# A graph network's first layer on one core: VectorE's mask, hits, small numbers and edge sources in a PSUM bank, and one bank for all sums by edge

## The reference, cut to what matters

```python
def _L0_gnn_ref(inp, edge_row, edge_col, edge_val, kernel, bias):
    support = jnp.matmul(inp, kernel)
    messages = edge_val[:, None] * support[edge_col]
    output = jax.ops.segment_sum(messages, edge_row, num_segments=N_NODES)
    return output + bias
...
x = _layernorm(x + _L0_gnn_ref(x, src, dst, edge_weight, L0_gnn_kernel, L0_gnn_bias), axis=-1)
x = _layernorm(x + _L1_gnn_ref(x, L1_gnn_bases, L1_gnn_relation_base_weights, src, dst, edge_type_64), axis=-1)
```

## Time and profile before

| | |
|---|---|
| median of 3 runs | 4513.46 us (4500.87 to 4518.20) |
| the profiled execution | 4505.52 us |
| its span in the profile | 4503.7 us |
| busy share of the span | PE 79%, DVE 56%, ACT 39%, POOL 60% |

### The profile page before, as it was taken

The page is one execution under the profiler, slowest core; times in us unless marked ns, Lnnn a source line. Parts: engine busy times, 40 slices in busy tenths (PEclk is TensorE's granted clock), DMA queues, the critical chain, the costliest instruction groups (busy, mean ns, idle before and its releaser), DMA issues. The chain is left out here.

```text
span 4503.7 us, 97674 instructions
## 1 busy us (share of the span) xinstructions
PE 3537.1 (79%) x24161; PEld 2643.1 (59%) x24162; DVE 2523.8 (56%) x8263; ACT 1765.9 (39%) x2669; POOL 2691.2 (60%) x2143
## 2 busy tenths in 40 slices
PE   4666767766777765377887877789999799989998
PEld 3444444444444443255555555578888688878886
DVE  7676767667676765555555555513333355545545
ACT  2555545555555553201111111146666434443342
POOL 2888888888888887777777777576666100000000
PEclk7878888787787887567677777689999899999999
DMA  7666666666666666522222222254444465665554
GB/s 266 140 126 142 132 134 136 130 139 127 140 131 138 133 137 139 159 57 62 62 65 64 64 61 64 62 163 135 130 138 131 170 215 197 211 227 184 203 192 156
DMA packets 364967, 615.01 MB, mean 137 GB/s; under 512 B 55224, under 2 KB 238689, under 8 KB 360752
## 3 DMA queue, kind: packets, MB, share of 16 engines
q1 hardware_dynamic: 151448, 340.06, 23.8%
q0 software_dynamic: 163968, 162.92, 21.0%
q10 hardware_dynamic: 49368, 110.28, 6.4%
HBM read 421.82 MB, written 194.63 MB: 137 GB/s over the span
## 5 line engine op out<-in xcount | busy, mean ns | idle before, releaser
L728 POOL DMA_INDIRECT rows<-t,idx_ring x1248 | 1193.3, 956 | 471.1 <-issue 389.1
L1403 PE MATMUL bank<-arena 128*128 128x384 bf16 (+1 forms) x2496 | 683.3, 413 | 490.7 <-DVE arena L2023 310.2
L1280 PE MATMUL bank<-alpha,arena 128*128 128x264 bf16 x7644 | 874.7, 277 | 14.3 <-ACT alpha L1105 10.1
L1280 PEld LDWEIGHTS bank<-alpha,arena 128*128 128x128 bf16 x7644 | 748.1, 98 | 131.1 <-issue 7.9
L768 POOL DMA_INDIRECT sums<-rows,idx_ring x416 | 729.5, 1754 | 152.2 <-issue 101.1
L768 POOL DMA_INDIRECT sums<-stage,idx_ring x416 | 708.2, 1702 | 132.2 <-issue 116.3
L893 ACT ACTIVATE node_data<-bank 128x384 f32 (+1 forms) x1248 | 576.7, 511 | 468.9 <-PE bank L1406 454.1
L1188 PE MATMUL bank<-S,rows 128*128 128x192 f32 (+1 forms) x2496 | 648.3, 399 | 19.6 <-DMA rows<-t,idx_ring 15.5
L1403 PEld LDWEIGHTS bank<-arena 128*128 128x128 bf16 x2496 | 175.1, 109 | 685.0 <-issue 418.4
L1188 PEld LDWEIGHTS bank<-S,rows 128*128 128x128 f32 x2496 | 477.7, 239 | 40.4 <-DMA rows<-t,idx_ring 15.9
L1304 PE MATMUL bank<-alpha,arena 128*128 128x264 bf16 x3822 | 447.7, 277 | 13.3 <-DMA arena<-xp 7.4
(11 more groups left out here) (220 smaller groups left out, 4768.5 us busy)
## 6 DMA issues: line engine op xcount, KB each, us to landing
shared<-adj SPq DMA_DIRECT2D x286, 462.0 KB, 3.5
adj<-node_data ACTq DMA_DIRECT2D x189, 462.0 KB
arena<-src_row SPq DMA_DIRECT2D x104, 512.0 KB
rows<-adj SPq DMA_DIRECT2D x104, 462.0 KB, 5.9
arena<-type SPq DMA_DIRECT2D x52, 512.0 KB
S<-adj SPq DMA_DIRECT2D x52, 462.0 KB, 6.6
rows<-t,idx_ring POOLq DMA_INDIRECT x1248, 2.5
arena<-xp POOLq DMA_DIRECT2D x14, 672.0 KB, 7.0
```

Source lines behind the costliest of these rows:

```text
L728: nc.gpsimd.indirect_dma_start(out=rows[:, k, t, :], out_offset=None, in_=tables[p], in_offset=bass.IndirectOffsetOnAxis(ap=idx_ring[:, j, ...
L1280: last = nc.tensor.matmul(bank[c][:, 0:CHUNK_COLS], x_parts[:, q * PIECE_H + hh, part, :], adj_slot[q][:, hh * CHUNK_COLS:(hh + 1) * CHUNK ...
L1403: nc.tensor.matmul(bank[bk][:, 0:(hb - ha) * W], lo, hw_hot[n * GT + t][:, ha * W:hb * W], start=t == 0, stop=False)
```

## The change

`hits` and a copy of the mask, of the numbers 0 to 23, and of a body's 16 columns of sources now lie in bank 1, whose 512 columns hold the mask (0 to 127), the numbers (128 to 151), `hits` (256 to 447, two steps' worth) and the sources (496 to 511). Mask and numbers are copied there once, before the loop (each copy waited for); the sources are copied in step 0 of each body, with a semaphore of their own (`src_ready`) that `sel` of that step waits for. `sel` now reads `src_rows` from SBUF and the sources from the bank, L2001 the mask from the bank, `hits` the numbers from the bank and `rel` from SBUF and writes to the bank, `wS` reads `hits` from the bank and `wgt` from SBUF. The sums by edge of all steps go to bank 0, and L1382 waits for the copy of step g-1 (`c_kept`, g + 2) in place of that of step g-2.

```diff
--- before.py
+++ after.py
@@ -196,7 +196,6 @@
         shared = sb("shared", [P, 2, 2, FT, P])
         sel = [shared[:, 0, s, :, :] for s in range(2)]
         masked = [shared[:, 1, s, :, :] for s in range(2)]
-        hits = sb("hits", [P, 2, FT, W])
         wS = sb("wS", [P, 2, FT, W])
         xwin = [[rows4[0:W, 2 + h, k, :] for h in range(FHALF)] for k in range(FSTEPS)]
         dup = sb("dup", [P, 2, FT])
@@ -328,6 +327,10 @@
         slow_G = sb("slow_G", [P, NB * W])
 
         bank = [ctx.enter_context(nc.psum_tensor(f"bank{k}", [P, 512], FP)) for k in range(8)]
+        earlier_0 = bank[1][:, 0:P]
+        iota_0 = bank[1][:, P:P + W]
+        hits = bank[1][:, 2 * P:2 * P + 2 * FT * W].rearrange("p (s t w) -> p s t w", s=2, t=FT)
+        src_0 = bank[1][:, 4 * P - BODY:4 * P]
         S01 = bank[5][:, 0:2 * PT * W].rearrange("p (k t w) -> p k t w", k=2, t=PT)
 
 
@@ -350,6 +353,7 @@
         types_in = sem("types_in")
         relw_ready = sem("relw_ready")
         hits_ready = sem("hits_ready")
+        src_ready = sem("src_ready")
         hot_ready = sem("hot_ready")
         alpha_summed = sem("alpha_summed")
         alpha_ready = sem("alpha_ready")
@@ -863,7 +867,7 @@
             def keep_window(i, k):
                 act.wait_ge(c_summed, i * FSTEPS + (k + 3))
                 act.wait_ge(messages, i * FSTEPS + (k + 3))
-                nc.scalar.activation(C[k % 2], bank[k % 2][0:W, :], ACT.Copy).then_inc(c_kept, 1)
+                nc.scalar.activation(C[k % 2], bank[0][0:W, :], ACT.Copy).then_inc(c_kept, 1)
 
             def keep_rows(i, k):
                 act.wait_ge(messages, i * FSTEPS + (k + 5))
@@ -1377,9 +1381,9 @@
             def window_by_edge(i, k):
                 g = i * FSTEPS + k
                 pe.wait_ge(sel_ready, g + (FSTEPS + 1))
-                pe.wait_ge(c_kept, g + 1)
+                pe.wait_ge(c_kept, g + 2)
                 for t in range(FT):
-                    last = nc.tensor.matmul(bank[k % 2][0:W, t * P:(t + 1) * P], wS[:, k % 2, t, :], sel[k % 2][:, t, :],
+                    last = nc.tensor.matmul(bank[0][0:W, t * P:(t + 1) * P], wS[:, k % 2, t, :], sel[k % 2][:, t, :],
                                             start=True, stop=True)
                 last.then_inc(c_summed, 1)
 
@@ -1932,6 +1936,8 @@
 
             dve.wait_ge(supported, NBLK)
             dve.wait_ge(scattered[1], 16)
+            after(nc.vector.tensor_copy(earlier_0, earlier[:, :]))
+            after(nc.vector.tensor_copy(iota_0, iota_w[:, :]))
             def typed_add(j):
 
                 at = dve.value_load(base_i[0:1, bass.ds(j * (2 * GPH) + GPH, 1)], min_val=0, max_val=N)
@@ -1985,12 +1991,16 @@
                     dve.wait_ge(c_summed, g + 1)
                     if k % 2 == 0:
                         dve.wait_ge(src_rows_in[k // 2], i * 16 + 16)
-                    nc.vector.tensor_tensor(hits[:, k % 2, :, :], iota_w[:, :].unsqueeze(1).to_broadcast([P, FT, W]),
+                    if k == 0:
+                        nc.vector.tensor_copy(src_0, src_f[:, bass.ds(i * BODY, BODY)]).then_inc(src_ready, 1)
+                    nc.vector.tensor_tensor(hits[:, k % 2, :, :], iota_0.unsqueeze(1).to_broadcast([P, FT, W]),
                                             rel[:, bass.ds(g * FT, FT)].unsqueeze(2).to_broadcast([P, FT, W]),
                                             ALU.is_equal).then_inc(hits_ready, 1)
                     at = k % 2 * (FT * P)
+                    if k == 0:
+                        dve.wait_ge(src_ready, i + 1)
                     nc.vector.tensor_tensor(sel[k % 2], src_rows[k // 2][:, at:at + FT * P].rearrange("p (t f) -> p t f", t=FT),
-                                            src_f[:, bass.ds(g * FT, FT)].unsqueeze(2).to_broadcast([P, FT, P]),
+                                            src_0[:, k * FT:(k + 1) * FT].unsqueeze(2).to_broadcast([P, FT, P]),
                                             ALU.is_equal)
                     dve.wait_ge(hits_ready, g + 1)
                     nc.vector.tensor_tensor(wS[:, k % 2, :, :], hits[:, k % 2, :, :],
@@ -1999,7 +2009,7 @@
                     dve.wait_ge(sel_ready, g + (FSTEPS + 1))
                     for t in range(FT):
                         last = nc.vector.tensor_tensor_reduce(
-                            out=masked[k % 2][:, t, :], in0=sel[k % 2][:, t, :], in1=earlier[:, :], scale=1.0, scalar=0.0,
+                            out=masked[k % 2][:, t, :], in0=sel[k % 2][:, t, :], in1=earlier_0, scale=1.0, scalar=0.0,
                             op0=ALU.mult, op1=ALU.add, accum_out=dup[:, k % 2, t:t + 1])
                     last.then_inc(dup_step, 1)
                     dve.wait_ge(dup_step, g * 3 + 1)
```

## The result

| | before | changed |
|---|---|---|
| median | 4513.60 us (4500.87 to 4518.20, 4 runs) | 4442.05 us (4436.86 to 4445.60, 4 runs) |
| ratio | | 0.9842 (95% interval 0.9825 to 0.9860) |
| the profiled execution | 4505.52 us | 4436.86 us |

The account below looks back on a forecast made before the run. GpSimd's scatters, one after another, were taken to bound the first layer's loop; 91 us less stretch minus 12 us of landing waits made 79 us, so 4513.5 - 79 = 4434 us, with a fast case of 4397 to 4499 us.

Parts of the forecast that it names:

- What bounds the loop: First layer's loop: GpSimd's scatters one after another, 8.18 us a step, against 6.40 us of VectorE's own.
- A bank operand frees GpSimd: Scatters beside L1988, L1992, L1996 and L2001: one SBUF tensor fewer there takes 91 us off the stretch.
- The chain of two-tensor operations until the fourth masked product: VectorE's L1988 to L2001: the chain keeps something from GpSimd until over; two scatters end 0.47 us after the fourth L2001.
- one that was held by L2001 alone ends at the same 0.47 us: Scatter of 1756.18: ends 0.47 us behind L2001, like that of 1747.37; used to choose 91 us over 35.
- The mixed class: 151 scatters beside both tensor_scalars and two-tensor operations: stretch falls from 0.506 to 0.110 us each, 60 us gained.
- Landings: Scatters wait for the one four before to land: these waits give back 12 us, between 0 and 30.
- Net: Whole kernel: 91 us gained less 12 us of landing waits, 79 us net.
- VectorE's prices: Bank operands and the 16-column copy cost VectorE 0.10 us a step, 21 us over 208 steps, hidden by its 369.5 us wait.
- One bank, prologue: L1382's wait for the copy of the step before, and copying mask and numbers before the loop: cost 0 each.
- the bank operand doesn't free GpSimd: Rival on the loop's scatters: stretch stays, time 4513 + 0 to 2 us; chance 0.10.

Follow-up runs that it names:

- e1_one_bank: The kernel before with only the sums by edge all put in bank 0, VectorE's operands staying in SBUF: ratio 1.0013 to the kernel before.
- e2_mask_only: The kernel before with one bank for the sums and only the mask in bank 1: ratio 1.0000 to the kernel before.
- e3_all_but_mask: The changed kernel with the mask back in SBUF, hits, numbers and sources in the bank: ratio 0.9886 to the kernel before.
- h1_changed_again: The changed kernel itself, repeated beside the kernel before on another chip: ratio 0.9879, 4851.1 us against 4910.0.
- g1_breaks: The kernel before with one bank for the sums and short maxima over an idle bank ahead of sel and wS: ratio 0.9938 to the kernel before.
- g3_types_low: The changed kernel with type one-hots comparing against a bank tensor and 128- and 49-column one-hots reading numbers from the bank: ratio 0.9839 to the kernel before.
- e6_low_numbers: The changed kernel with numbers 0 to 127 in the bank for the 128- and 49-column one-hots: ratio 0.9844 to the kernel before.

## Why the prediction was right, and where it was not

- **What bounds the loop: right.** GpSimd's scatters, before and after; VectorE waits for them in both, and the rest of the run stayed (2713.75 us for 2714.7).
- **A bank operand frees GpSimd: right.** The scatters beside products alone went from 31 us of stretch to 0.4, as forecast, and none of 2.75 us is left. e1_one_bank, e2_mask_only and e3_all_but_mask put it down to `hits`, `sel` and `wS`.
- **"The chain of two-tensor operations until the fourth masked product": wrong in its end.** The step that failed is "one that was held by L2001 alone ends at the same 0.47 us". The hold ends with `wS`; the masked products and the mask's copy have no part that the runs can tell. That it did no harm to the sum is luck: all parts were changed together. Of the mask alone the same reading forecast 40 to 65 us, and 0 came.
- **The mixed class: mis-sized.** It was to fall to the 0.110 us of scatters beside tensor_scalars alone, 17 us left; it kept 0.202 us, 32.5 us. The average over all such scatters was the wrong row: in this class the type one-hot stands just where it catches one, 81 scatters of 0.26 us each. The prediction had ruled it out because it ended 0.39 us into the scatter of 1747.37; by the 1.43 us behind its end that gives 1.82 us, and 1.81 was measured. With this, GpSimd gained 76.9 us and not 91.
- **Landings: right in kind, smaller in size.** 8.9 us came back against 12, and 16 us in the profile of h1_changed_again.
- **Net.** 76.9 - 8.9 = 68 us in the loop for 79; loop 1632.7 us for 1622; time 4442 us for 4434. VectorE's wait is 301 us for 270, of which 11 us are the longer loop.
- **VectorE's prices: right or too high.** `hits` 24 ns for 17, `sel`, `wS` and masked products 0 or a few ns less for 6 each, the copy 165 ns for 197. The Trainium skill ("VectorE: DVE Perf Modes", TRN2 errata) charges a PSUM source 62 cycles more than an SBUF one; the rows of `sel` (670 ns for 678) and of the masked products (283 for 288), which each read one operand from the bank and one from SBUF, do not agree, and the measurement decides.
- **One bank, prologue: right**, 0 by e1_one_bank and by the first row of the table.
- **The rival "the bank operand doesn't free GpSimd"** is out. Behind it stood the Trainium skill's remark ("SBUF — State Buffer", "Who interferes with whom") that a `tensor_tensor` was not seen to stall a DMA; here products with two SBUF operands stretched GpSimd's indirect DMAs by up to 0.57 us alone, and by 0.94 us more behind a type one-hot (2.75 us for 1.81), and those with one did not. With its other rule, that a VectorE instruction with two SBUF inputs contends with a GpSimd instruction that reads SBUF, this agrees; which access of GpSimd's it is, no run shows.

## What to carry to other kernels

Where GpSimd's DMA issues are the bound, sort them by duration and look up which VectorE instruction ends at a fixed distance before each long one's end; a distance that repeats to 0.02 us over a hundred cases names the holder, one that was seen twice can name its neighbour. Then take one SBUF operand away from the middle of VectorE's longest back-to-back run: that gives most of the gain (61 of 68 us here, by a 16-column copy each body), and a bank operand cost these products nothing that the rows show. Ask next what waits behind the freed engine: here 20 us more freed bought 2 to 12 us, about what two profiles differ by.

## What the runs showed of the hardware that was not expected

- A scatter held by the products lasts to 1.43 or 1.44 us behind the end of their whole unbroken run, not of one instruction. A type one-hot (32-bit numbers to bf16) directly ahead belongs to it: in the scatters of 2.75 us the run goes from 0.35 us ahead of the scatter to 1.32 us into it. Among the one-hots it is not so. Of the 105 scatters of the changed kernel that end 1.44 us behind a 1176-column one-hot, 69 are let go while a 128-column one-hot follows without a pause, and 36 while a 49-column one does, a kind that itself ends 88 holds. Why is not shown. Since a free scatter takes 1.55 us, what a held one waits for would come some 0.12 us in, an estimate; which part of GpSimd's work asks is not shown.
- An instruction of 0.17 us on bank operands between two of the run is enough to let the scatter through (g1_breaks).
- VectorE seems to be held in its turn. In the changed kernel 81 of the 824 one-hots of 1176 columns take over 0.56 us (the median is 0.52), and all 81 end 0.19 or 0.23 us before a scatter does, as here (GpSimd, then VectorE; 601.73 for 601.95). In g3_types_low these are 198, and their mean, all 824 taken together, goes from 531 to 572 ns. No run tried this by itself.

```profile
600.40 1.55 POOL L772 DMA_INDIRECT sums<-rows,idx_ring  x1 [0.30 <-issue]
```

```profile
600.93 0.80 DVE L2032 TENSOR_SCALAR arena<-S 128x1176 bf16<-128x1176 int16 x1
```

- The masked products, whose operands all lay in SBUF and which also run for a microsecond, hold a scatter only a little: in e3_all_but_mask the scatters beside products alone average 1.567 us and take 1.62 at most, with the mask in the bank 1.552 (changed kernel). An accumulator read stands behind each of them (82 ns); that it breaks the run is a guess that fits g1_breaks.
- The tensor_scalar of 128 columns takes 402 ns in e6_low_numbers, with 32-bit numbers in the bank, where it took 333 with 16-bit numbers in SBUF; place and type changed together, and which of them costs it is open. The 49-column one, changed in the same way, takes 260 ns for 263.

```profile
L2031 DVE TENSOR_SCALAR arena<-bank,arena,hot_at 128x128 bf16<-128x128 f32 x824 | 331.0, 402 | 72.7 <-issue 66.5 <-PE bank L1411 6.0
```
